# Three score pairs in a row: regrouping TensorE's work in an attention loop, and turning the row maxima in the score banks

## The reference

```python
Q = (x @ Wq.T + bq).reshape(B, S, H, Hd).transpose(0, 2, 1, 3)
K = (x @ Wk.T + bk).reshape(B, S, H, Hd).transpose(0, 2, 1, 3)
V = (x @ Wv.T + bv).reshape(B, S, H, Hd).transpose(0, 2, 1, 3)
scores = jnp.einsum('bhqd,bhkd->bhqk', Q, K) / jnp.sqrt(jnp.float32(Hd))
attn = jax.nn.softmax(scores, axis=-1)
out = jnp.einsum('bhqk,bhkd->bhqd', attn, V)
return out.transpose(0, 2, 1, 3).reshape(B, S, D) @ Wo.T + bo
...
x = x + attention(layernorm(x))      # this layer
x = x + ffn(layernorm(x))            # silu gate, Hadamard transform, down
x = x + memory(layernorm(x))         # gated scan over the tokens
x = x + ffn(layernorm(x))
```

## Time and profile before

| | us |
|---|---|
| median of 3 runs (lowest, highest) | 586.15 (585.88, 586.72) |
| the profiled execution, its own time | 586.26 |
| its span in the trace | 584.4 |
| TensorE busy | 565.8 (97%) |
| VectorE busy | 376.8 (64%) |
| ScalarE busy | 298.5 (51%) |
| the loop of 128 steps, in the trace | about 46 to 252 |

### The profile page before, as it was taken

The page is one execution under the profiler, slowest core; times in us unless marked ns, Lnnn a source line. Parts: engine busy times, 40 slices in busy tenths (PEclk is TensorE's granted clock), DMA queues, the critical chain, the costliest instruction groups (busy, mean ns, idle before and its releaser), DMA issues.

```text
span 584.4 us, 8867 instructions
## 1 busy us (share of the span) xinstructions
PE 565.8 (97%) x3288; PEld 390.1 (67%) x3288; DVE 376.8 (64%) x718; ACT 298.5 (51%) x546; POOL 176.6 (30%) x193
## 2 busy tenths in 40 slices
PE   9899999999999988999999999999999999999997
PEld 4534334344334433368888888898777888888886
DVE  5498898898888899644363444558887436344433
ACT  3238878876886787752334242244445233424221
POOL 3956446354455242820101010014333010101000
PEclk9999999999999999999999999999999999999999
DMA  7654740240033030010000000000000010010101
GB/s 231 135 112 163 199 122 18 76 127 20 2 111 109 3 146 3 3 72 2 1 0 1 1 0 1 2 2 0 1 0 2 1 36 1 1 36 2 38 0 37
DMA packets 17891, 26.54 MB, mean 45 GB/s; under 512 B 2552, under 2 KB 10744, under 8 KB 17464
## 3 DMA queue, kind: packets, MB, share of 16 engines
q1 hardware_dynamic: 15992, 24.13, 13.6%
q10 hardware_dynamic: 1856, 1.84, 1.4%
HBM read 10.88 MB, written 5.24 MB: 28 GB/s over the span
## 4 chain that ended last, share of the span: by engine, by line
PE 85%; DVE 5%; ACT 4%; issue 2%; DMA 1%; POOL 1%; SPq 1%; DVEq 0%; ACTq 0%
PE PS L281 82%; PE PS L292 2%; DVE mxr L861 2%; ACT PR L735 1%; DMA ring<-ql 1%; DVE PR L1020 1%; ACT xf L644 1%; ACT qf L658 1%; DVE XNs L842 1%; ACT PR L788 1%; POOL xTl L1051 1%; ACT xTh L644 1%; PE PS L472 1%; DVE AOl L853 1%; SPq L214 1%
## 5 line engine op out<-in xcount | busy, mean ns | idle before, releaser
L281 PE MATMUL PS<-xTh,ring 128*128 128x512 f32 x608 | 188.5, 392 | 0.0
L861 DVE TENSOR_REDUCE mxr<-PS 128x1 f32<-128x512 f32 x256 | 163.0, 682 | 29.0 <-PE PS L281 28.7
L735 ACT ACTIVATE PR<-PS 128x512 f32<-128x512 f32 x256 | 137.8, 603 | 39.7 <-PE PS L281 39.7
L281 PEld LDWEIGHTS PS<-xTh,ring 128*128 128x128 f32 x608 | 113.2, 188 | 22.9 <-issue 0.8
L281 PE MATMUL PS<-xTl,ring 128*128 128x512 f32 x304 | 110.3, 391 | 0.4 <-POOL xTl L1051 0.4
L281 PE MATMUL PS<-ring 50*128 50x512 f32 (+1 forms) x512 | 98.2, 450 | 5.4 <-DVE mxr L861 4.9
L975 DVE TENSOR_TENSOR PR<-PR,PS 128x512 f32<-128x512 f32 x64 | 43.8, 684 | 91.6 <-PE PS L281 73.7
L281 PEld LDWEIGHTS PS<-ring 50*128 50x128 f32 (+1 forms) x512 | 41.2, 184 | 84.2 <-ACT PR L735 57.2
L644 ACT ACTIVATE AOh<-PR 128x512 fp32r<-128x512 f32 x72 | 45.5, 632 | 101.1 <-DVE PR L975 89.2
L1051 POOL TENSOR_TENSOR xTl<-xf,xTh 128x512 fp32r<-128x512 f32 x30 | 43.2, 1456 | 140.9 <-ACT xTh L644 140.9
L853 DVE TENSOR_TENSOR AOl<-PR,AOh 128x512 fp32r<-128x512 f32 x72 | 51.1, 710 | 50.3 <-ACT AOh L644 50.3
(11 more groups left out here) (98 smaller groups left out, 621.5 us busy)
## 6 DMA issues: line engine op xcount, KB each, us to landing
ring<-qh SPq DMA_DIRECT2D x52, 128.0 KB, 3.1
ring<-ql SPq DMA_DIRECT2D x26, 128.0 KB, 3.1
ring<-weight_scratch SPq DMA_DIRECT2D x3, 1024.0 KB, 4.9
weight_scratch<-in_w SPq DMA_DIRECT2D x2, 1024.0 KB, 6.8
out<-X SPq DMA_DIRECT2D x8, 256.0 KB, 2.2
X<-in_x SPq DMA_DIRECT2D x3, 512.0 KB, 5.2
PR<-in_w SPq DMA_DIRECT2D x1, 1024.0 KB, 7.6
ring<-AOh SPq DMA_DIRECT2D x8, 128.0 KB, 4.0
```

What stands on the lines that cost most here:

```text
L281: return nc.tensor.matmul(dst, lhsT, rhs, start=start, stop=stop, skip_group_check=True)
L735: nc.scalar.activation(PR[:, j % 8, :], PS[:, kq_bank(j), :], ACT.Exp, scale=HD ** -0.5)\
L861: nc.vector.tensor_reduce(mxr[:, S % 2, blk, TT * p + t:TT * p + t + 1], PS[:, QK0 + i % 3, :], AX.X, ALU.max, negate=True).then_inc(max_d ...
```

## The change

Three things change on TensorE, and one operand on ScalarE and VectorE.

1. The loop runs over pairs j, not over steps. After every third pair there is a gap, and in it stands the work of the steps due by then: `gap_of(K)`. With K = 3m, 3m+1, 3m+2 the gaps are after pairs 6m+2, 6m+2 and 6m+5. So gaps alternate between the work of two steps (3m and 3m+1) and of one (3m+2). For K = 3m+1 the gap lies between the two pairs of its own step.
2. The turn no longer goes to bank 7. It takes a place of its own in the rotation of banks 3 to 5 (`slots`): it waits for the maximum three places before it, and the pair three places after it waits for `mt_ready`, that is, for ScalarE's copy to `mT`.
3. Waits on bank 7 in `shared_bank` no longer name the turn, only the copy before.

```diff
-TAIL_BANKS = (2, 4, 5, 3, 0, 1)
+TAIL_BANKS = (2, 3, 4, 5, 0, 1)
+
+RUN = 3
...
+        def gap_of(K):
+
+            return (2 * K + 2 - (RUN - 1)) // RUN * RUN + RUN - 1 if RUN > 1 else 2 * K
+
+
+        turn_gap = {S: gap_of(8 * (S - 1) + MAX_AT) for S in range(1, LAST_GROUP - 1)}
+        slots = [("score", i) for i in range(2 * LEAD)]
+        for pair in range(TAIL):
+            slots.append(("score", pair + 2 * LEAD))
+            slots += [("turn", S) for S, gap in turn_gap.items() if gap == pair]
+        slot_of = {what: n for n, what in enumerate(slots)}
+
+        def qk_bank(i):
+            return QK0 + slot_of["score", i] % 3
+
+        def turn_bank(S):
+
+            return PS[:, QK0 + slot_of["turn", S] % 3, :] if S in turn_gap else MB
...
+            def wait_slot(n):
+
+                if n >= 3:
+                    kind, i = slots[n - 3]
+                    pe.wait_ge(max_done if kind == "score" else mt_ready, i + 1)
+
+            def turn_max(S):
+                pe.wait_ge(ml_done, S + 1)
+                pe.wait_ge(mt_ready, S)
+                if S in turn_gap:
+                    wait_slot(slot_of["turn", S])
+                else:
+
+                    pe.wait_ge(x_done, 2 * BATCH - 3)
+                nc.tensor.transpose(turn_bank(S)[0:32, 0:P], ms[:, :, :, :].rearrange("p a b k -> p (a b k)"),
+                                    ident[:, :]).then_inc(mps_ready, 1)
...
-                if 2 * U + h >= 3:
-                    pe.wait_ge(max_done, 2 * U + h - 2)
+                wait_slot(slot_of["score", 2 * U + h])
...
-            for K in range(STEPS * BATCH):
-                b, s = K // STEPS, K % STEPS
-                for h in range(2):
-                    wait_kq(K, h)
-                    if K + LEAD < STEPS * BATCH:
-                        wait_qk(K + LEAD, h)
-                    score_kq(K, h)
-                    if K + LEAD < STEPS * BATCH:
-                        score_qk(K + LEAD, h)
-
-                shared_bank(K, b, s)
-                if K % 2 and K >= 3:
-                    weigh_values((K - 3) // 2)
+            for j in range(2 * STEPS * BATCH):
+                K, h = j // 2, j % 2
+                wait_kq(K, h)
+                if K + LEAD < STEPS * BATCH:
+                    wait_qk(K + LEAD, h)
+                score_kq(K, h)
+                if K + LEAD < STEPS * BATCH:
+                    score_qk(K + LEAD, h)
+
+                for k in range(max(K - 2, 0), K + 1):
+                    if gap_of(k) == j:
+                        shared_bank(k, k // STEPS, k % STEPS)
+                        S = (k + LEAD) // 8 - 1
+                        if k % 8 == MAX_AT and S < LAST_GROUP:
+                            turn_max(S)
+                        if k % 2 and k >= 3:
+                            weigh_values((k - 3) // 2)
```

More of the change, by code:

```diff
@@ L339, in score_qk @@
                 r = HALF * blk
-                mm(PS[:, QK0 + i % 3, :], ring[r:r + KROWS, b % 2, QI, p, t * P:(t + 1) * P],
+                mm(PS[:, qk_bank(i), :], ring[r:r + KROWS, b % 2, QI, p, t * P:(t + 1) * P],
                    ring[r:r + KROWS, b % 2, KI, p, :], True, True).then_inc(s1_ready, 1)
@@ L364, in wait_kq @@
                 if TAIL < j < TAIL + 4:
-                    pe.wait_ge(max_done, 2 * STEPS * BATCH - 3 + j - TAIL)
+                    wait_slot(len(slots) - 1 + j - TAIL)
                 elif j > TAIL:
@@ L444, in shared_bank @@
             def shared_bank(K, b, s):
-                more, turned = b < BATCH - 1, K + LEAD
+                more = b < BATCH - 1
                 if s == LN_AT[0] and more:
                     pe.wait_ge(xns_ready, b + 2)
-                    pe.wait_ge(mt_ready, turned // 8)
+                    pe.wait_ge(v_copied, 2 * (b + 2))
                     ln_transpose(0, MB)
@@ L454, in shared_bank @@
                     ln_transpose(1, MB)
[L455 to L473, removed]
                 for n in range(4):
@@ L478, in shared_bank @@
                                 pe.wait_ge(x_f, 2 * (b + 1))
-                            elif n == 2:
-                                pe.wait_ge(qk_f, 4 * b + 2)
                             else:
-                                pe.wait_ge(mt_ready, turned // 8)
+                                pe.wait_ge(qk_f, 4 * b + n)
                         i = 3 * QK_AT[n].index(s)
@@ L489, in shared_bank @@
                     else:
-                        pe.wait_ge(mt_ready, turned // 8)
+                        pe.wait_ge(x_f, 2 * (b + 1))
                     for part in range(2):
@@ L493, in shared_bank @@
                 if s in OUT_AT[1] and b:
-                    if s == OUT_AT[1][0]:
-                        pe.wait_ge(mt_ready, turned // 8)
+                    if s == OUT_AT[1][0] and more:
+                        pe.wait_ge(v_copied, 2 * (b + 1) + 1)
+                    elif s == OUT_AT[1][0]:
+                        pe.wait_ge(mt_ready, LAST_GROUP)
                     out_projection(1, OUT_AT[1].index(s))
@@ L507, in shared_bank @@
                     elif s == V_AT[1][0]:
-                        pe.wait_ge(mt_ready, turned // 8)
+                        pe.wait_ge(v_copied, 3)
                     project_v(b + 1, 1, V_AT[1].index(s))
-            for K in range(STEPS * BATCH):
-                b, s = K // STEPS, K % STEPS
-                for h in range(2):
-                    wait_kq(K, h)
-                    if K + LEAD < STEPS * BATCH:
-                        wait_qk(K + LEAD, h)
-                    score_kq(K, h)
-                    if K + LEAD < STEPS * BATCH:
-                        score_qk(K + LEAD, h)
-                shared_bank(K, b, s)
-                if K % 2 and K >= 3:
-                    weigh_values((K - 3) // 2)
+            for j in range(2 * STEPS * BATCH):
[14 more added lines that the diff above has]
+                            weigh_values((k - 3) // 2)
+            for k in range(STEPS * BATCH - 2, STEPS * BATCH):
+                if gap_of(k) >= 2 * STEPS * BATCH and k % 2:
+                    weigh_values((k - 3) // 2)
             weigh_values(STEPS * BATCH // 2 - 1)
@@ L674, in max_evacuate @@
                     act.wait_ge(mrow_in, 2 * DMA * S)
-                hi(mT[:, :], MB[0:32, 0:P]).then_inc(mt_ready, 1)
+                hi(mT[:, :], turn_bank(S)[0:32, 0:P]).then_inc(mt_ready, 1)
             for t in range(2, TT):
@@ L860, in row_max @@
                     dve.wait_ge(ml_done, S - 1)
-                nc.vector.tensor_reduce(mxr[:, S % 2, blk, TT * p + t:TT * p + t + 1], PS[:, QK0 + i % 3, :], AX.X,
+                nc.vector.tensor_reduce(mxr[:, S % 2, blk, TT * p + t:TT * p + t + 1], PS[:, qk_bank(i), :], AX.X,
                                         ALU.max, negate=True).then_inc(max_done, 1)
```

## The result

| | before | after |
|---|---|---|
| median, us (4 runs each) | 586.25 | 606.25 |
| lowest, highest | 585.88, 586.72 | 600.88, 608.18 |
| the profiled execution: own time, span | 586.26, 584.4 | 608.18, 606.4 |

The ratio is 1.0329, 95% interval 1.0299 to 1.036: slower by 20.0 us, where 13.3 was forecast. The time lies 0.25 us above the top of the range. New, too, is the spread of 7.3 us between executions. Each execution has a mean granted clock of TensorE: 1.0 in the one of 600.88, and 0.985, 0.988 and 0.985 in those of 608.18, 605.51 and 606.98.

The account below looks back on a forecast made before the run. TensorE, 97% busy, was taken to bound the loop, paying 0.18 us per run of pairs. 8.3 us removed and 21.6 added gave +13.3, so 599.5 us median, range 584.5 to 606 (main case's own range 592 to 606).

Parts of the forecast that it names:

- (a): Third pair behind a single gap waits for its bank, double gaps cost nothing: 22 places, 7.1 us added.
- (c): Turns of steps K = 3m+1: third pair waits for ScalarE's copy, the next run's for the DMA's rows: 7.9 us added.
- (b): VectorE's and ScalarE's other work between first and third maximum before a single gap: 2.8 us added, bounds 0 and 5.6.
- the 1.3 of step 109: Share of (c) for the last batch's turn, with no gap work but VectorE as the bound: 1.3 us.
- (d): Other turns, right behind their run, wait for its first maximum, 1.41 against 0.90: eight times 0.3, 2.4 us added.
- The runs to remove: Steps 0 to 95: 93 runs become 64, saving 5.2 us; three joined places of four pairs save 2.1 us.
- the 1.0 of the waits: TensorE's turn waiting for bank 7, which the change was to remove: 1.0 us saved.
- between 0 and -1: Last batch: VectorE sets the pace of four pairs and a weighing before and after; 0 taken.
- Boundaries win: Rival: only TensorE's count of groups matters, and meeting pieces spare 0.1 each: 4.9 us faster, 581.2; chance 0.17.
- It cancels: Rival: (c) at its lower bound, (b) and (d) nothing, meeting pieces spare 3.2: 587 us; chance 0.08.
- Landing at every turn: Rival: rows come late for the other eight turns too, some 0.8 each: 606 us; chance 0.05 shared with another rival.
- The signs: Profile: TensorE's maxima waits 4.9 to over 15 us, five `mT` or DMA waits, VectorE idle up by the loop's growth.

Follow-up runs that it names:

- e1: Changed kernel with runs of two pairs instead of three, the turn still in the score banks: 583.83 us, ratio 0.9965 to the kernel before.
- e2: Changed kernel with runs of three, but the turn back in bank 7 with the earlier waits: 608.11 us, ratio 1.0366 to the kernel before.
- e10: Changed kernel with ScalarE's turn copy earlier, maxima over 256 of 512 keys and exponentials over 256 of 512 columns: 577.69 us, ratio 0.9843 to the kernel before.
- e11: Kernel before with maxima over 256 keys and exponentials over 256 columns, control for e10: 578.69 us, ratio 0.9877.
- e9: Changed kernel with ScalarE's turn copy earlier and maxima over 256 of 512 keys: 586.15 us, ratio 1.0009 to the kernel before.
- e3: Changed kernel with ScalarE's copy of the K = 3m+1 turns behind the step's first exponential, not the second: 597.66 us, ratio 1.0188 to the kernel before.
- e4: Changed kernel with the early turn copy and runs of 3, 3 and 2 pairs per four steps: 590.57 us, ratio 1.0084 to the kernel before.
- e8: Changed kernel with runs of four pairs, each followed by two steps' work, no turn between its step's pairs: 616.76 us, ratio 1.0528 to the kernel before.

## Why the prediction was right, and what it missed

**The mechanism** was the predicted one. The third pair came 2.57 us behind the start of the last run, against 2.63, the turn at 1.41 against 1.41, and the landing at 3.93 against 3.93. Runs of two with the same turn lose nothing (e1), runs of three lose in either bank (e2), and shorter consumers take most of the cost away (e10 against e11). One rule of (a) held in the main only. Of the 20 runs behind a gap of two pieces, with no turn of (c) in it and no turn behind the run, 16 took 0.89 to 0.91, but four took 1.09 to 1.12. The first of them, with VectorE's work ahead of it, and in the same timeline a run with VectorE's work inside it:

```profile
62.07 0.72 DVE L929 STREAM_TRANSPOSE OT<-PS 128x512 f32<-128x512 f32 x1 [0.51 <-PE PS L302]
...
62.84 1.18 PE L302 MATMUL PS<-ring 50*128 50x512 f32 x6
...
195.98 0.67 DVE L946 TENSOR_TENSOR X<-X,PS 128x512 f32<-128x512 f32 x1
...
197.40 0.50 PE L302 MATMUL PS<-ring 50*128 50x512 f32 x2 [0.67 <-DVE mxr L886]
```

At 62.07 VectorE has waited 0.51 for the weighing of the gap, because its program has the transpose of bank 6 ahead of the last run's third maximum. That maximum comes after it, and the run at 62.84 takes 1.11. At 195.98 an addition stands between two maxima of the run of 194.10, and the next run's third pair starts 3.30 behind that run, not 2.63: this is (b).

**The sum**, set against the one run at a full clock, is off by little: 600.88 less 586.25 is 14.6, and 13.3 was forecast. Runs at one clock lie up to 2.3 us apart (e9), so this is no closer than that. By stretches of the profiled execution: batches 0 to 2, from layer norm to layer norm, grew from 161.0 to 174.1 us. Of that 1.5 is the clock (0.86 in the weighing, 0.39 in the transposes, the rest in the pair), so 11.6 is the change, where the prediction had 12.0 (13.3 less the 1.3 of step 109). The last batch grew by 7.9 us. Its four slowed weighings and a turn alone lost 3.3 of that to the clock; with the early copy, at a full clock, it grew by 2.1. The 0.9 us left stands ahead of the layer norm of batch 0 and differs among the kernels (e3 has -0.4); its cause stays open.

**The step that failed** is one that isn't in the prediction: that the earlier trace rows would keep their prices. They were taken at a granted clock of 1.0, and in the changed kernel that clock was gone for 17 us. At the median this is 606.25 - 600.88 = 5.4 us, counted from a single run at the full clock, and the difference within e4 (3 to 6 us at 0.991 to 0.988) says the same of another kernel. So the median came to the range's top, 606, by a term that the sum, with its own high end of 604, doesn't have. That the standstills bring the falls is shown in part: filling ten of them removed two of three falls in the profile, and brought the clocks of the four runs to 0.994 to 0.997, where the changed kernel had one at 1.0 and three at 0.985 to 0.988. Against it as the whole cause: the same pairs of waits passed elsewhere without a fall, e8 waits most and falls little, and e4 had a fall ahead of the loop. Where they come differs from kernel to kernel, and how many from run to run.

**Terms that were off and cancelled.** That 12.0 met 11.6 is in part luck: both sides were some 2 us short. Counted from 0.90 for each run of three, the runs before took 12.1 us more (69.7, where 64 times 0.90 is 57.6), where the prediction's terms give 10.0, and the runs after 23.9 more (81.8, with the clock's 0.3 taken off), where they give 22.0. (Both forecasts are counted with a turn's full 1.41; (d) itself had taken off 0.2 for each of its eight turns, which were late before.)
- The runs to remove: 92, with four joined places, not 93 with three (steps 1 and 2 are joined too). Two more runs of two, at 142.74 and 197.25, took 0.99 before.
- The turn's lateness: (d) and the 1.0 of the waits had it together, 2.7, and it was 2.7 (0.94 or 0.95 and 0.85 against 0.67). The expectation of e1 took only the part that the waits name, and so 0.9 in place of 2.0. The turn of step 101, in the last batch, is in no term of (d).
- (a) and (b), 9.9 together, were low: 11.6. The twelve runs behind a lone weighing of (a) are 0.37 too long where 0.26 was priced, from 0.11 to 0.93. What is over goes with VectorE's work, (b), which was taken at half of its bound, and with the four runs behind two pieces (0.8); the split between the two terms stays open.
- (c), 7.9, was right in size (7.1 for the four turns of batches 0 to 2, where 6.6 was forecast) and wrong as a separable price. Taking the copy ahead gave 3.9 to 5.0 us: it was one of two waits in a row, and behind it stand the landing and ScalarE's splits, which were hidden by it.
- The last batch, "between 0 and -1": it was +2.1 even in e3, where step 109's turn is copied early. The turns of steps 101 and 109 now stand 1.41 behind their runs, which may be part of it; no run says what the rest is.

**The rivals.** "Boundaries win" decides at the round trip, and the traces have that at its forecast length. Once the consumers are short a lone weighing costs nothing, as its rule has it, but even e10 gained only 1.0 of its 5, and that with the turn moved. That two pieces meeting spare something isn't seen: half a projection and a weighing take 0.90 + 1.00 side by side (from 112.65 to 113.54 and to 114.54 in e10). "It cancels" is out by the same. "Landing at every turn" gave 606, nearly the measured time, by a cause that isn't there: only four waits for the DMA, 2.1 us. A number that fits is no evidence.

**The signs** named ahead: waits for maxima of over 15 us in some 25 new places are 9.4 us in 17 (5.5 for pairs, 3.9 for turns), by that sign too few, since many stalls hide in a modelled end. The waits for `mT` or its DMA came ten times, 6.5 us, where five were named: two for each of the four turns of (c) in batches 0 to 2, one at step 109 and one, of 1.0, for the turn of step 117, which waited 0.4 before too. VectorE's idle time (19.2 us more for an execution 22.0 longer) and the stretch behind the loop came about as forecast.

Still open: what exactly makes the clock fall; why the first landing in e10 keeps TensorE for 1.62 us and the three later ones for 1.2 together; and what e4 would be with ScalarE's splits moved.

## What to carry to other kernels

A saving per group (here 0.18 us for each run of pairs) is bounded by the buffers: with three banks and a round trip of 1.41 us for one, 2.6 for three, runs of two are the longest that any gap covers, and no kernel here with longer runs gained more over its control than moving the turn into the banks' own rotation did alone (2.0 us). Before stretching a group, put the round trip of its last buffer against the shortest gap, and look at which in-order work of the consumers falls between. Then ask whether the new waits come close together, because the clock may fall behind short stalls, which costs more than their own length.

## What the runs showed of the hardware beyond what was expected

TensorE's granted clock fell to 1.2 GHz for 3.4 or 6.8 us at a time, in a loop in which it was in flight for 95% of a middle batch and 86% of most of the last, after standstills of 0.4 to 1.4 us that came close together. It did so in some executions of a program and not in others: 600.88 at 1.0 and 608.18 at 0.985 for the same kernel, 588.64 at 1.0 and 594.55 at 0.988 in e4. Such standstills didn't always bring a fall: two pairs of them passed in the same execution, and e8, with 51 waits of up to 0.9 us for maxima and exponentials, had one fall of 3.4 us. The kernel before, with 11 waits for maxima of 0.6 us at most, showed 0.999 or 1.0 in its runs, but for one of 0.996 (beside e1).
